# ScalarE instead of VectorE normalises the next sample's x, in exchange for one copy per sample

## The reference, cut to what matters

```python
def _ln(x):
    m = jnp.mean(x, axis=-1, keepdims=True)
    v = jnp.var(x, axis=-1, keepdims=True)
    return (x - m) / jnp.sqrt(v + EPS)
x = _ln(src) * (1.0 + scale) + shift            # scale, shift: one row per sample
q = (x @ Wq + bq).reshape(B, S, N_HEAD, HEAD_DIM).transpose(0, 2, 1, 3)   # k, v alike
scores = jnp.einsum('bhqd,bhkd->bhqk', q / math.sqrt(HEAD_DIM), k)
scores = scores + attention_bias                # 8 x 16 x 512 x 512, from HBM
scores = jnp.where(src_mask, -jnp.inf, scores.astype(jnp.float32))
probs = jax.nn.softmax(scores, axis=-1)
ctx = jnp.einsum('bhqk,bhkd->bhqd', probs, v)
x = x + (ctx @ Wo + bo)
h = _ln(x) * g2 + beta2
ff = _gelu2(h @ W1 + b1) @ W2 + b2              # x + ff goes on to the adapters
```

## Time and profile before

| | us |
|---|---|
| runs (3): median, lowest, highest | 979.27, 978.79, 980.8 |
| profiled execution, its own time | 979.03 |
| its span, first to last instruction | 977.2 |
| busy: PE, DVE, ACT, POOL | 933.8, 736.0, 671.1, 711.4 |

### The profile page before, as it was taken

The page is one execution under the profiler, slowest core; times in us unless marked ns, Lnnn a source line. Parts: engine busy times, 40 slices in busy tenths (PEclk is TensorE's granted clock), DMA queues, the critical chain, the costliest instruction groups (busy, mean ns, idle before and its releaser), DMA issues. The chain is left out here.

```text
span 977.2 us, 20035 instructions
## 1 busy us (share of the span) xinstructions
PE 933.8 (96%) x5838; PEld 614.7 (63%) x5838; DVE 736.0 (75%) x1987; ACT 671.1 (69%) x1120; POOL 711.4 (73%) x570
## 2 busy tenths in 40 slices
PE   5889999999999999999999999989899999999996
PEld 5656556656656665665675566555477777777574
DVE  8877887879869788887976978787445675668566
ACT  3576878898788787879878878888544354444333
POOL 1789789788878878978896897888454455557465
PEclk9989999999999999999999999999999999999998
DMA  8988998997997899699789879985211110111101
GB/s 298 334 313 282 382 326 274 339 374 244 323 389 281 291 375 363 237 342 387 263 295 390 306 272 363 356 266 180 87 44 44 44 44 22 44 66 44 44 23 64
DMA packets 127533, 229.96 MB, mean 235 GB/s; under 512 B 6512, under 2 KB 53872, under 8 KB 123632
## 3 DMA queue, kind: packets, MB, share of 16 engines
q1 hardware_dynamic: 127472, 229.26, 66.0%
HBM read 187.30 MB, written 41.94 MB: 235 GB/s over the span
## 5 line engine op out<-in xcount | busy, mean ns | idle before, releaser
L944 ACT ACTIVATE prob<-prob,nmax 128x512 f32<-128x512 f32 x512 | 358.2, 729 | 63.5 <-DVE nmax L765 59.8
L765 DVE CUSTOM_DVE_ANT_0 prob<-s_bank,big 128x512 f32<-128x512 f32 x512 | 339.2, 686 | 76.2 <-POOL big L1118 41.4
L596 PEld LDWEIGHTS t_bank<-ident,prob 128*128 128x128 f32 x2048 | 239.5, 141 | 161.8 <-issue 45.3
L596 PE MATMUL t_bank<-ident,prob 128*128 128x128 f32 x2048 | 317.5, 278 | 11.6 <-ACT pt L951 4.8
L1118 POOL TENSOR_TENSOR big<-big,mterm_early 128x2048 f32<-128x2048 f32 (+2 forms) x78 | 271.0, 3490 | 44.7 <-DMA big<-in_fside_Bx16xSxS 28.4
L951 ACT COPY pt<-t_bank 128x512 f32<-128x512 f32 x314 | 183.1, 585 | 44.3 <-PE t_bank L596 43.0
L584 PE MATMUL s_bank<-stack_k,stack_q 128*128 128x512 bf16 x512 | 195.7, 382 | 3.4 <-DVE nmax L765 3.2
L774 DVE COPY pt<-t_bank 128x512 f32<-128x512 f32 x198 | 136.1, 687 | 30.3 <-PE t_bank L596 30.0
L610 PE MATMUL o_bank<-pt,val 128*32 128x512 f32 x1024 | 123.2, 599 | 0.9 <-ACT pt L951 0.7
L2223 POOL TENSOR_TENSOR gl<-big,gh 128x512 fp32r<-128x512 f32 x64 | 83.1, 1306 | 49.0 <-DVE gh L1765 49.0
L2074 ACT ACTIVATE big<-bank,late 128x512 f32<-128x512 f32 x62 | 42.6, 689 | 72.6 <-PE bank L1472 69.1
(11 more groups left out here) (249 smaller groups left out, 1473.1 us busy)
## 6 DMA issues: line engine op xcount, KB each, us to landing
big<-in_fside_Bx16xSxS SPq DMA_DIRECT2D x128, 1024.0 KB, 7.7
pieces_dram<-pieces SPq DMA_DIRECT2D x64, 384.0 KB, 6.9
stack_q<-pieces_dram SPq DMA_DIRECT2D x15, 1024.0 KB, 8.1
stack_k<-pieces_dram SPq DMA_DIRECT2D x15, 1024.0 KB, 9.7
pieces_dram<-pieces SPq DMA_DIRECT2D x32, 256.0 KB, 7.3
xin<-in_x SPq DMA_DIRECT2D x8, 512.0 KB, 8.8
x_dram<-x SPq DMA_DIRECT2D x8, 512.0 KB, 4.2
x1r<-x_dram SPq DMA_DIRECT2D x8, 512.0 KB, 4.5
```

The lines of the kernel that those rows point to most:

```text
L596: last = pe.transpose(t_bank[n % 2][:, c * P:(c + 1) * P], prob[:, n % NT, c * P:(c + 1) * P], ident[:])
L765: dve.tensor_tensor_reduce(out=prob[:, n % NT, :], in0=s_bank[n % 3][:, :], in1=bias[:, h % NB, t, :], scale=-1.0, scalar=3e38, op0=ALU.ad ...
L944: act.activation(tile, tile, ACT.Exp, bias=nmax[:, n % NT:n % NT + 1], scale=-1.0).then_inc(exped.sem, 1)
```

## The change

The normalisation of the next sample's x moves from VectorE (n = 14) to ScalarE, right behind the two instructions of `deviation` (n = 12). ScalarE computes func(scale * x + bias), so it needs minus mean times 1 / deviation as a bias: `less_mean` is made beside the logarithm, `less_scaled` behind the exponential by four instructions of one column each, and then four instructions write `xin`. In exchange VectorE copies the turned tile 13. In the last sample, where no next x exists, tile 13 stays ScalarE's; there VectorE now copies tiles 61 and 63 where it copied 62.

The last sample's own layer norm (another use of `normalise`, on VectorE) and the one ahead of the first sample stay where they are, but `deviation` has the added instruction there too.

```diff
-STATISTICS_AT, DEVIATION_AT, NORMALISE_AT = 11, 12, 14
+STATISTICS_AT, DEVIATION_AT = 11, 12
...
-DVE_TAKES = (3, 7, 8, 12, 14, 17, 21, 22, 23, 25, 27, 30, 31, 34, 35, 36, 38, 40, 44, 46, 49, 51, 55, 57, 60)
-DVE_TAKES_LAST = tuple(n for n in DVE_TAKES if n not in (21, 22, 25)) + (62,)
+DVE_TAKES = (3, 7, 8, 12, 13, 14, 17, 21, 22, 23, 25, 27, 30, 31, 34, 35, 36, 38, 40, 44, 46, 49, 51, 55, 57, 60)
+DVE_TAKES_LAST = tuple(n for n in DVE_TAKES if n not in (13, 21, 22, 25)) + (61, 63)
...
-        std_done, log_done = (Count(sem(n), 1, 1) for n in ("std_done", "log_done"))
+        std_done, log_done = Count(sem("std_done"), 1, 1), Count(sem("log_done"), 2, 2)
+        factors_done = Count(sem("factors_done"), 1, 0)
+        less_mean, less_scaled = sb("less_mean", [P, QT]), sb("less_scaled", [P, QT])
...
-                    if not last and n == NORMALISE_AT:
-                        normalise(b)
...
                 act.activation(std[:], mv[:, :, 1], ACT.Ln, bias=eps[:, 0:1]).then_inc(log_done.sem, 1)
-                act.wait_ge(log_done.sem, log_done.at(b, 1))
+                act.activation(less_mean[:], mv[:, :, 0], ACT.Identity, scale=-1.0).then_inc(log_done.sem, 1)
+                act.wait_ge(log_done.sem, log_done.at(b, 2))
                 act.activation(rstd[:], std[:], ACT.Exp, scale=-0.5).then_inc(std_done.sem, 1)
+
+            def normalise(b):
+                act.wait_ge(std_done.sem, std_done.at(b, 1))
+                for t in range(QT):
+                    last = act.activation(less_scaled[:, t:t + 1], less_mean[:, t:t + 1], ACT.Identity, scale=rstd[:, t:t + 1])
+                last.then_inc(factors_done.sem, 1)
+                act.wait_ge(factors_done.sem, factors_done.at(b, 1))
+                for t in range(QT):
+                    last = act.activation(xin[:, t], xin[:, t], ACT.Identity, bias=less_scaled[:, t:t + 1], scale=rstd[:, t:t + 1])
+                last.then_inc(xhat_done.sem, 1)
...
                     if n == (DEVIATION_LAST if last else DEVIATION_AT):
                         deviation(b)
+                        if not last:
+                            normalise(b)
```

## The result

| | kernel before | changed kernel |
|---|---|---|
| median (range), 6 runs each | 979.1 us (977.7 to 980.8) | 987.39 us (985.8 to 988.0) |
| ratio, 95% interval | | 1.0082 (1.007 to 1.0094) |
| profiled execution, its span | 979.03, 977.23 us | 987.09, 985.28 us |

One run of experiment 7 (1194.88 us, at a granted clock of 0.75) was a slow one and is left out of its figures.

The account below looks back on a forecast made before the run. The prediction took PE to set the pace; +2.6 us (samples 1 to 6), +0.4 (sample 0) and -0.1 (the end) make +2.9 on 979.03, so 981.9 us, range 976.5 to 986.5.

Parts of the forecast that it names:

- ScalarE's block: ScalarE's added instructions ahead of exponential 14: that exponential can start 3.71 us after the logarithm starts.
- TensorE at turn 15: Transposes of xin and turn 15, samples 1 to 6: PE 0.65 us late per sample, +2.6 us in sum.
- The transposes' wait: PE's transposes of xin waiting for DVE's normalisation, worth 0.71 us in sample 3, would be gained.
- The first sample and the end: Sample 0, transposes one group later at the lower clock: +0.4 us; last sample's copies 61 and 63: -0.1 us.
- DVE's chain gains 0.76 us: DVE loses four normalising instructions and gains one copy, so its residual starts 0.76 us earlier per sample.
- so I cost the gain on DVE and POOL at nothing: DVE's wait for POOL's addition 36 is covered by busy PE, so the 0.76 us gain counts as zero.
- What PE loses here comes back at the end in full: From sample 6: PE 0.50 us later at the normalisation, sample 82.96 us against a mean of 82.03.
- DVE and POOL set the pace: Rival: less DVE work ahead of the residual brings addition 36 forward; seven samples gain 5.3 us, 973.7; chance 0.10.
- longer block: Rival: ScalarE's added instructions take longer, exponential 14 starts 4.7 us after the logarithm, PE 1.65 late; 988.8 us; chance 0.10.
- The clock falls: Rival: PE standing still about 1 us before turn 14 lowers the granted clock in samples 1 to 6; +20, 1002; chance 0.06.

Follow-up runs that it names:

- experiment 7: Changed kernel with ScalarE's scaled means and normalising instructions behind exponential 15, and the transposes of xin behind turns 15 and 16: 986.96 us, ratio 1.0086.
- Experiments 1 to 3: Changed kernel with extra GpSimd work: 980.97 us; changed kernel with a GpSimd wait: 981.03 us; kernel before with half the late mask term left out: 985.26 us.
- experiment 2: Changed kernel, GpSimd begins its mask addition of head 7 only when VectorE has made both low parts: 981.03 us, ratio 1.0026 to the kernel before.
- experiment 5: Changed kernel with ScalarE's scaled means and normalising instructions moved behind exponential 14: 976.97 us, ratio 0.9977 to the kernel before.
- experiments 6 to 8: Changed kernel: normalising behind exponential 14, tile 13 on ScalarE, 986.8 us; behind exponential 15, transposes at 15, 16, 986.96; behind 16, transposes at 16, 17, 1023.38.

## Why the prediction was wrong

- *ScalarE's block*: right. 3.59 us, forecast 3.71; `less_scaled` 0.85 for four (0.20 apart, as taken), the normalising instructions 0.50 apart (taken 0.51).
- *TensorE at turn 15*: right, +2.6 us over six samples. The transposes' wait is gone, turn 14 is 1.31 late (forecast 1.36).
- *The first sample and the end*: +0.4 forecast, 0.19 measured up to the start of sample 1; -0.1 forecast, -0.06 to turn 63.
- *"DVE's chain gains 0.76 us", "so I cost the gain on DVE and POOL at nothing"*: this step failed. I asked whether a gain on GpSimd could help, found it covered, and took covered for harmless. It moves GpSimd against TensorE, by my two own numbers: 0.76 earlier and 0.65 later make 1.41, and the trace has 1.36 (the mask addition that precedes the late mask term starts 7.97 us ahead of turn 20, 6.61 before). The low parts move with TensorE, the masks with GpSimd. The late mask term then runs clear of the low parts, which saves 2 x 0.32 us more. So the mask addition moved by 1.99 us against turn 20, while it stood 1.65 us behind the start of the second low part (315.07 against 313.42). The 1.41 alone would not have closed that margin; with the 0.64 it is closed. Experiments 1 to 3 show the price: 6 us.
- *"What PE loses here comes back at the end in full"*: sample 6 was no witness for this change. Its slow normalisation holds up the transposes and the residual alike, so TensorE and GpSimd are late together: the mask addition of head 7 starts 1.00 us behind turn 20 there, and 1.00 to 1.02 in samples 1 to 5. The change makes one late and the other early. Also, 0.5 of its 0.93 us lie behind turn 36, not at this place.
- *The rivals*: none had this. "DVE and POOL set the pace" saw their gain as good or nothing. The price of the "longer block" (988.8) was near the result by luck: the block was not longer (3.59 us). "The clock falls" did not happen, 1.00 in samples 1 to 6. Its argument misread sample 0: by the trace the granted clock is 0.97 from 53.0 to 53.5 us and 0.50 from there, so it fell during the wait of 2.06 us that ended at 54.35, not behind it.

The Trainium skill (SBUF — State Buffer, sections SBUF: two separate sides and Who interferes with whom) says that a VectorE instruction with two SBUF inputs contends with a GpSimd instruction that reads SBUF, and that whichever starts first keeps the shared port pair for its whole instruction while the other fully blocks. The traces agree: the second low part ends 0.54 to 0.56 us behind the GpSimd instruction that started first, whether that is 0.94, 2.45 or 4.5 us long. The signs were in the trace before: a low part of 1.09 beside one of about 0.7, mask terms of 0.94 beside 0.62, and a normalisation of 1.95 beside one of 1.45. By that rule, the two shifts and the time that the mask term instructions save when they run clear, the collision could be forecast.

What stays open: why turn 15 to 20 is 0.15 us shorter with the block behind exponential 14 (7.77), and the 1.0 us that came back elsewhere; neither was tested.

## What to carry to other kernels

An engine whose lateness TensorE does not feel is not free to move. When a change makes one chain earlier and another later, add both shifts, and go through the pairs of instructions that were seen to wait for each other across the two chains: here VectorE's low parts and normalisation, and GpSimd's mask instructions. An instruction that is sometimes longer than its like (1.09 for 0.68) marks such a pair, and the distance to GpSimd's next long instruction is the margin. If it must hold, a wait on the engine with slack holds it (experiment 2: some 6 us for one line). And ScalarE's new work was cheaper behind an exponential that was done 1.8 us early than in front of it (experiment 5), but each such move shifts the margin again: experiments 6 to 8 lost it.

## What the runs showed of the hardware

- A GpSimd tensor_tensor and a VectorE tensor_tensor, both with two SBUF inputs, run one behind the other: a low part took 0.68 us with GpSimd idle, 1.09 beside a tensor_scalar of GpSimd, 2.62 beside its addition of 128x1024, and 4.54 beside one of 128x2048. GpSimd pays too when VectorE starts first: 0.94 for 0.62, 2.45 for 2.15.
- VectorE's tensor_scalar from SBUF to SBUF (the normalisation, 128x256 f32) waits likewise: 0.47 to 0.98 for the one that started inside a mask addition, 0.40 for the next three. VectorE's bias additions (scores from PSUM, bias from SBUF) do not: in the kernel before they took 0.66 to 0.70 us, all 512, and 219 of them lay wholly inside a tensor_tensor of GpSimd.
- The one that waits is charged the whole time in its own busy row. DVE looked busier by 2.4 us over samples 1 to 6 (410.74 for 408.35) although it had less to do; the list of what DVE waited for in the changed kernel has no row for the low parts.
- ScalarE's Identity with pointer scale and bias, 256 columns from SBUF to SBUF: 2.08 us for four, 0.50 apart. One column with a pointer scale: 0.85 for four, 0.20 apart.
